# An attention block with adaptive layer norm on one core: the value products in blocks of four steps, the turned maxima behind a block, and low parts formed from PSUM

## The reference, cut to what matters

```python
sa, ca, ga, sb, cb, gb = silu(c) @ wmod           # six vectors of 256 per batch; ga, gb kept away from 0
h = layernorm(x) * (1 + ca) + sa
q, kv = h @ Wq.T, h @ Wkv_down.T                  # 8 heads of 64; keys and values come from a latent of 64
k, v = kv @ Wk_up.T, kv @ Wv_up.T
x = x + ga * (softmax(q k / 8) v) @ Wo.T          # per head, 1024 x 1024 scores
h2 = layernorm(x) * (1 + cb) + sb
x = x + gb * (h2 @ weight.T + pooled(h2) @ disha)
```

## Time and profile before, and how to read it

| | |
|---|---|
| median of 3 runs | 3259.14 us (3256.48 to 3263.53) |
| the profiled execution: its own time, its span | 3262.56 us, 3260.8 us |
| TensorE matmul, busy | 3175.0 us, 97% of the span |
| VectorE, ScalarE, GpSimd, busy | 67%, 52%, 79% |
| chain that ended last: TensorE's share | 92% |

### The profile page before, as it was taken

How to read it: one execution, slowest core, us unless ns; L and a number is a source line. 1 busy time by engine, 2 the same in 40 slices (tenths; PEclk the granted TensorE clock), 3 DMA queues, 4 the chain that set the end, 5 groups by cost and what they waited for, 6 DMA issues and landing times.

```text
span 3260.8 us, 44881 instructions
## 1 busy us (share of the span) xinstructions
PE 3175.0 (97%) x15398; PEld 1927.1 (59%) x15398; DVE 2200.4 (67%) x2542; ACT 1705.1 (52%) x3203; POOL 2584.8 (79%) x1513
## 2 busy tenths in 40 slices
PE   5999999999999999999999999999999999999995
PEld 3555656566566665665666565665656656666554
DVE  4657676776767767677776767767677776766652
ACT  1555555555555555555555555555555555555451
POOL 1778788887888878788887878878788887877882
PEclk7999999999999999999999999999999999999995
DMA  2111111111112011121111112111110111111111
GB/s 68 40 44 55 46 66 33 49 60 47 56 47 66 31 58 53 47 66 33 53 56 47 56 47 66 35 55 52 47 66 34 53 56 46 56 46 53 43 34 36
DMA packets 161746, 163.16 MB, mean 50 GB/s; under 512 B 58480, under 2 KB 109808, under 8 KB 161520
## 3 DMA queue, kind: packets, MB, share of 16 engines
q1 hardware_dynamic: 161520, 160.30, 15.0%
HBM read 74.66 MB, written 17.33 MB: 28 GB/s over the span
## 4 chain that ended last, share of the span: by engine, by line
PE 92%; DVE 5%; POOL 1%; issue 1%; ACT 1%; DMA 1%; SPq 0%; POOLq 0%; ACTq 0%; DVEq 0%
PE ps_mix L547 27%; PE ps_score L565 16%; PE ps_max L586 14%; PE ps_score L567 14%; PE ps_side L535 6%; PE ps_side L646 6%; PE ps_side L664 3%; PE ps_side L633 2%; DVE neg_max L984 1%; DVE w_out_lo L993 1%; POOL prob_sum L842 1%; PE ps_side L604 1%; DVE query L1027 1%; PE ps_side L653 1%; DVE h_lo L1017 1%
## 5 line engine op out<-in xcount | busy, mean ns | idle before, releaser
L842 POOL TENSOR_TENSOR prob_sum<-prob_sum,probs 128x1024 f32<-128x1024 f32 x768 | 1881.0, 2449 | 243.4 <-ACT probs L722 188.2
L984 DVE TENSOR_REDUCE neg_max<-ps_max 128x1 f32<-128x1024 f32 x1024 | 1247.9, 1220 | 755.3 <-PE ps_max L586 749.3
L722 ACT ACTIVATE probs<-ps_score 128x512 f32<-128x512 f32 x2048 | 1113.3, 598 | 969.0 <-PE ps_score L567 956.5
L547 PE MATMUL ps_mix<-probs,values 128*64 128x512 f32 x4096 | 991.6, 605 | 0.0
L565 PE MATMUL ps_score<-query,key_hi 128*128 128x512 f32 x2048 | 873.7, 427 | 1.1 <-ACT probs L722 1.1
L567 PE MATMUL ps_score<-query_m,key_lo 128*128 128x512 f32 x2048 | 805.0, 393 | 0.0
L586 PE MATMUL ps_max<-key_hi,query 128*128 128x512 f32 x2048 | 644.5, 396 | 8.3 <-DVE neg_max L984 5.4
L565 PEld LDWEIGHTS ps_score<-query,key_hi 128*128 128x128 f32 x2048 | 384.6, 188 | 326.7 <-issue 246.2
L547 PEld LDWEIGHTS ps_mix<-probs,values 128*64 128x64 f32 x4096 | 248.4, 136 | 477.8 <-issue 477.1
L842 POOL TENSOR_TENSOR prob_sum<-probs 128x1024 f32<-128x1024 f32 x128 | 328.9, 2570 | 228.6 <-ACT probs L722 228.3
L586 PEld LDWEIGHTS ps_max<-key_hi,query 128*128 128x128 f32 x2048 | 386.2, 189 | 102.3 <-DVE neg_max L984 10.9
(11 more groups left out here) (119 smaller groups left out, 2907.5 us busy)
## 6 DMA issues: line engine op xcount, KB each, us to landing
query_m<-query SPq DMA_DIRECT2D x128, 512.0 KB, 3.2
recip<-recip_scratch SPq DMA_DIRECT2D x256, 128.0 KB, 2.9
x_in<-in_L_attn_x_dram SPq DMA_DIRECT2D x32, 512.0 KB, 4.0
x_mid<-in_L_attn_x_dram SPq DMA_DIRECT2D x64, 256.0 KB, 4.5
out_dram<-x_mid SPq DMA_DIRECT2D x64, 256.0 KB, 2.2
denoms<-recip SPq DMA_DIRECT2D x512, 1.0 KB, 1.7
gates<-gates_scratch SPq DMA_DIRECT2D x16, 256.0 KB, 4.1
query_m<-max_row SPq DMA_DIRECT2D x128, 4.0 KB
```

The source lines that it names most:

```text
L547: last = nc.tensor.matmul(ps_mix[j * R:j * R + R, :], values[par][:, k, :], probs[:, s % RING, j * HALF:(j + 1) * HALF], start=(k == 0), s ...
L722: nc.scalar.activation(probs[:, s % RING, half * HALF:(half + 1) * HALF], ps_score[half], ACT.Exp, scale=SCALE).then_inc(exps_done, 1)
L842: nc.gpsimd.tensor_tensor(out=total[:, :], in0=before, in1=probs[:, s % RING, :], op=ALU.add).then_inc(adds_done, 1)
L984: nc.vector.tensor_reduce(neg_max[:, m:m + 1], ps_max[m % 2][:, :], AX_X, ALU.max, negate=True).then_inc(maxima_done, 1)
```

## The change

- `MIXED` goes from 2 to 4: the products of four steps run together, in the steps 1, 5, 9, ... of a slot, and there are 16 blocks in a slot instead of 32. `RING` goes from 4 to 6.
- `max_row` goes from the steps 1, 9, 17, ... to 5, 13, 21, ... (four steps later in a group), `denominator` from 3, 11, ... to 1, 9, ... (two steps earlier); `MIX_LAG` goes from 5 to 4. Both stand in a step with a block, as before.
- `norm_t`: ScalarE now writes `h_hi` and then, from SBUF, `h_rest` = shift - `h_hi`; VectorE forms `h_lo` = scale * PSUM + `h_rest` in the same step and frees `ps_side`. `norm2_t` likewise: two activations for `h2_hi`, two for `h2_rest`, then two operations of VectorE. The pieces `h2_split`, L1008, L1017 and `split_h2` are gone.
- Places in `PLAN` move: `norm_t` to (8, 12, 16, 20), `out_proj` to (10, 14, 18, 22, ...), `mixed_hi` to (6, 15, 24, 40), `norm2` to (18, 26, 38, 50), and the gating of the `ffn` weights to the steps 2, 3 and 5. `query`, `latent`, `values_t`, `norm2_t` and `ffn` keep their steps.
- The two `mixed` buffers become one of 11 rows, which the batches use in turn from either end; the weights staged at the start go to other tiles.

```diff
-RING = 4
+RING = 6
-SPREAD_LAG, RECIP_LAG, OUT_LAG, BACK_LAG, MIX_LAG = 1, 2, 2, 3, 5
-MIXED = 2
+SPREAD_LAG, RECIP_LAG, OUT_LAG, BACK_LAG, MIX_LAG = 1, 2, 2, 3, 4
+MIXED = 4
-OUT_GATES_LOAD, OUT_GATE, OUT_HI, OUT_LO = 44, 52, 54, (56, 59)
-FFN_GATE, FFN_HI, FFN_LO = (1, 8), (3, 9), (7, 11)
+OUT_GATES_LOAD, OUT_GATE, OUT_HI, OUT_LO = 44, 52, 54, (57, 61)
+FFN_GATE, FFN_HI, FFN_LO = (1, 2), (3, 3), (7, 5)
     "query": (40, 42, 50, 58, STEPS, STEPS + 2, STEPS + 4, STEPS + 6),
-    "norm_t": (8, 10, 16, 18),
+    "norm_t": (8, 12, 16, 20),
     "latent": (26, 32),
     "values_t": (54, 60),
-    "mixed_hi": (9, 16, 24, 40),
-    "mixed_lo": (10, 17, 25, 41),
-    "out_proj": (12, 14, 20, 22, 30, 36, 44, 46),
-    "norm2": (16, 25, 38, 49),
+    "mixed_hi": (6, 15, 24, 40),
+    "mixed_lo": (9, 17, 25, 41),
+    "out_proj": (10, 14, 18, 22, 30, 36, 44, 46),
+    "norm2": (18, 26, 38, 50),
     "norm2_t": (24, 34, 48, 56),
-    "h2_split": (25, 35, 49, 57),
     "ffn": (28, 38, 52, 62),
...
-        "max_row": STEPS - NT + 1 + NT * i,
-        "denominator": NT * (i + 1) + 3,
+        "max_row": STEPS - NT + 5 + NT * i,
+        "denominator": NT * (i + 1) + 1,
...
                         elif kind == "norm_t":
...
-                            for part, done in ((h_hi[:, f, cols], h_hi_done), (h_whole[:, i % 2, :], side_drained)):
-                                nc.scalar.activation(part, ps_side[:, :], ACT.Identity,
-                                                     scale=mod1[:, f:f + 1], bias=mod1[:, NF + f:NF + f + 1]).then_inc(done, 1)
+                            nc.scalar.activation(h_hi[:, f, cols], ps_side[:, :], ACT.Identity,
+                                                 scale=mod1[:, f:f + 1], bias=shift).then_inc(h_hi_done, 1)
+                            need_alone(act, h_hi_done, 2 * (2 * NF * b + i) + 1)
+                            nc.scalar.activation(h_rest[:, i % 2, :], h_hi[:, f, cols].bitcast(F32), ACT.Identity,
+                                                 scale=-1.0, bias=shift).then_inc(h_hi_done, 1)
...
                             for f in range(NF):
-                                last = nc.scalar.activation(h2_t[:, f, :], ps_side[:, f * CT * P:(f + 1) * CT * P], ACT.Identity,
-                                                            scale=mod2[:, f:f + 1], bias=mod2[:, NF + f:NF + f + 1])
-                            last.then_inc(side_drained, 1)
+                                nc.scalar.activation(h2_hi[:, f, :], ps_side[:, f * CT * P:(f + 1) * CT * P], ACT.Identity,
+                                                     scale=mod2[:, f:f + 1], bias=mod2[:, NF + f:NF + f + 1]).then_inc(h2_hi_done, 1)
+                            for f in range(NF):
+                                need_alone(act, h2_hi_done, 2 * NF * (CHUNKS * b + i) + NF + f)
+                                nc.scalar.activation(h2_rest[:, f, :], h2_hi[:, f, :].bitcast(F32), ACT.Identity,
+                                                     scale=-1.0, bias=mod2[:, NF + f:NF + f + 1]).then_inc(h2_hi_done, 1)
...
+                        elif kind == "norm2_t":
+                            need(dve, h2_hi_done, 2 * NF * (CHUNKS * b + i + 1))
+                            for f in range(NF):
+                                last = nc.vector.scalar_tensor_tensor(h2_lo[:, f, :], ps_side[:, f * CT * P:(f + 1) * CT * P],
+                                                                      mod2[:, f:f + 1], h2_rest[:, f, :], ALU.mult, ALU.add)
+                            last.then_inc(side_drained, 1)
```

More of the change, by code:

```diff
@@ L256, in adaln_block @@
         prob_total = recip
-        mixed = [sb(f"mixed{i}", [P, PAIRS, T]) for i in range(2)]
+        mixed = sb("mixed", [P, 2 * PAIRS + 3, HALF])
         mixed_hi = sb("mixed_hi", [P, PAIRS, CT * P], F32R)
@@ L606, in side_work @@
                     elif kind == "latent":
-                        need(pe, h_split, 2 * NF * b + NF * (i + 1))
+                        need(pe, side_drained, z.through("norm_t", NF * i + 1) + 1)
                         if first(z):
@@ L655, in side_work @@
                     elif kind == "ffn":
-                        need(pe, h2_split, CHUNKS * b + i + 1)
+                        need(pe, side_drained, z.through("norm2_t", i) + 1)
                         if i == 0:
@@ L700, in _ @@
             nc.scalar.activation(s_silu[:, 0, :, :], s_c, ACT.Exp, scale=-1.0).then_inc(exp_c_made, 1)
[L702 to L706, removed]
             act.wait_ge(fold_a_kept, 8)
@@ L728, in slot @@
                         need(act, group_done, GROUPS * zg.c + g + 1)
-                        nc.scalar.activation(mixed[zg.par][:, p, half * HALF:(half + 1) * HALF], ps_mix[:, :],
+                        if zg.has_o and p > half:
+                            need(act, mixed_split, CHUNKS * zg.o + 2 * (half + 1))
+                        nc.scalar.activation(mixed_block(zg.par, p, half), ps_mix[:, :],
                                              ACT.Copy).then_inc(group_evacuated, 1)
@@ L840, in add_probs @@
                     need(pool, adds_done, done)
-                before = probs[:, (s - 1) % RING, :] if k == 1 else total[:, :]
-                nc.gpsimd.tensor_tensor(out=total[:, :], in0=before, in1=probs[:, s % RING, :], op=ALU.add).then_inc(adds_done, 1)
+                now = STEPS * z.c + s
+                before = probs[:, (now - 1) % RING, :] if k == 1 else total[:, :]
+                nc.gpsimd.tensor_tensor(out=total[:, :], in0=before, in1=probs[:, now % RING, :], op=ALU.add).then_inc(adds_done, 1)
             def slot(z):
@@ L1013, in slot @@
                         statistics(z.n + 1, 0, AHEAD_STATS.index(s))
-                    for g in range(CHUNKS):
-                        if z.has_o and s == z.step("h2_split", g):
-                            need(dve, h2_hi_done, CHUNKS * z.o + g + 1)
-                            nc.vector.tensor_tensor(h2_lo[:, :, :], h2_t[:, :, :], h2_hi[:, :, :].bitcast(F32),
-                                                    ALU.subtract).then_inc(h2_split, 1)
                     for kind, i, b, w in z.at(s):
@@ L1034, in slot @@
                                                     key_hi[1 - z.par][:, cols].bitcast(F32), ALU.subtract).then_inc(side_drained, 1)
+                        elif kind == "norm_t":
+                            need(dve, h_hi_done, 2 * (2 * NF * b + i + 1))
+                            half, f = divmod(i, NF)
+                            cols = slice(half * HALF, (half + 1) * HALF)
+                            nc.vector.scalar_tensor_tensor(h_lo[:, f, cols], ps_side[:, :], mod1[:, f:f + 1], h_rest[:, i % 2, :],
+                                                           ALU.mult, ALU.add).then_inc(side_drained, 1)
+                        elif kind == "norm2_t":
[4 more added lines that the diff above has]
+                            last.then_inc(side_drained, 1)
                         elif kind == "out_proj":
```

46 lines of the change are left out of this document (20 added, 26 removed).

## The result

| | before | after |
|---|---|---|
| median (4 runs each, one chip) | 3261.34 us (3256.48 to 3263.89) | 3328.93 us (3322.27 to 3336.40) |
| ratio, 95% interval | | 1.021 [1.0183, 1.0237] |
| profiled execution: its own time, its span | 3262.56, 3260.8 us | 3336.40, 3334.6 us |

The change makes the kernel 68 us slower by the medians and 73.8 by the spans. The prediction had the sign, and its range (3224 to 3335) holds the time, but its size was +32 where +68 came.

The account below looks back on a forecast made before the run. TensorE, busy 97% of the span, bounds the kernel. Terms -88 -6 +62 +8 +8 +29 +3 +6 +10 sum to +32 us, 3291 us median; ends -5 to +70, own range 3255 to 3330, full range 3224 to 3335.

Parts of the forecast that it names:

- Part 1: TensorE's product blocks: two blocks in one save 0.35 us, over 252 blocks, -88 us.
- the hold-back of the first score matmul: After a wait, the first score matmul holds the second back by 0.34 us instead of 0.23: 0.11 per late drain.
- Part 2: Scores wait for ScalarE's exponentials where no block follows: query +62, latent +8, values +8, `norm2_t` +29, `mixed_hi` +3 us.
- `mixed_hi` at step 15 (+3): ScalarE's 1.06 us copy between exponentials, mostly covered by step 16's transposes: 0.2 us, 15 times, +3 us (0 to 9).
- The step that failed first: Steps with `out_proj` and `ffn`: VectorE drains them, they take 1.4 us of TensorE, nothing late; no cost.
- The step that failed second: Scaling at `MIX_LAG` 4 may hold VectorE, but the maxima queued behind have 3.6 us of cover; no cost.
- Part 3: Denominators two steps earlier use up group 6's 6.07 us margin: +6 us (0 to 15); an old query-drain wait goes: -6 us.
- Part 4: Low parts on VectorE: worth nothing in a slot; `ps_side` held longer at start and tail, +10 us (2 to 16).
- Rival B: GpSimd holds the steps; two groups a slot wait 2 us for additions, 60 us more: 3350; B and C together 0.12.
- A: Rival: late exponentials are absorbed, only saved blocks and small terms remain: -75 us, 3184 us; chance 0.12.
- A': Rival: late exponentials are partly absorbed, half the price: 3238 us; chance 0.12.
- C: Rival: blocks of four save only half and the waits stay: 44 us more, 3335; B and C together 0.12.

Follow-up runs that it names:

- Experiments 2 and 3: 2: changed kernel with five pairs of places exchanged, 3269.24 us; 3: changed kernel with an unused third copy of PSUM by ScalarE for five queries, 3368.82 us.
- experiment 6: Changed kernel with the low part of the ffn weights (`w_ffn_lo`) at step 13 instead of 5: 3325.72 us, ratio 1.02 to the kernel before.
- experiment 9: Changed kernel with blocks of two and the earlier kernel's places and lags, keeping low parts, ring of six, one `mixed` buffer: 3342.79 us, ratio 1.024.

## Why the prediction was right in sign and wrong in size

- **Part 1, blocks**: right where it was read. A block of four takes 3.65 us, and blocks with their ends save 60 us against 63.
- **Part 1 and 2, the hold-back of the first score matmul**: wrong by 9 us. I let each saved block save 0.1 and charged it back only behind late drains. It came back in the plain steps too: the second matmul starts over 0.29 us behind the first 43 times a slot, before and after alike.
- **Part 2, late exponentials**: right. Forecast and measured waits: query 0.69 and 0.70 to 0.72 (0.85 at step 8), latent 0.43 and 0.45, values 0.43 and 0.5, `norm2_t` 1.84 and 1.73. `mixed_hi` at step 15 (+3) shows nothing beyond the wait of a plain step. Experiments 2 and 3 confirm them from either side.
- **The step that failed first**: "`out_proj` and `ffn` are drained by VectorE ...: nothing late there". Nothing is late, but scores, exponential and scores again close in 1.38 us, and the step offers 1.39. The missing cover costs 0.08 of wait six times a slot, 7.8 us in the run, and most of the 9 us of hold-back above: some 17 us.
- **The step that failed second**: the scaling "may hold VectorE, but ... the maxima queued behind it have 3.6 us of cover". I did not add up what stands in that queue: two operations of 2.9 us. The transposes lose 7.6 us to it (experiment 6 takes them away), and the maxima of the steps 0, 8 and 48 about 8 more to VectorE (at the turn to slot 3 to the scaling's DMA and `w_out_lo`; the other slots' queues are not taken apart): 16 us. At a lag of four steps the scaling also waits 205.5 us for the reciprocals' DMA, 122 times, where it waited 12.9, four times.
- **Part 3, denominators**: the mechanism was right, the term mis-sized: 0.9 us a slot instead of 0.4. The new wait is 13.7 us where 6 were forecast, and the old one that goes is 7.8 where 6 were forecast: +6 instead of 0. Rival B was this wait at 2 us for two groups; it came at one group and under half the size.
- **Part 4**: nothing in a slot and 6.6 us at the start, as forecast (the tail gave nothing). But "worth nothing" holds behind the long blocks and in the new places; with blocks of two in the old places the same edit costs 78 us (experiment 9), which I had not seen.
- **The ends of the range**: the ends that stand with the terms add up to +1 and +62; the -5 and +70 of the sum have no working. That 3329 lies within the range owes to this width and to rival B's, not to the terms.
- **The rivals**: A and A' fell on the waits of step 4, 36 and the rest; C fell on the block's 3.65 us.

What stays open: why the wait of a plain step is there behind some pieces (the steps 16, 24, 32, 40, 48 and 0) and not behind others (12 and 20), and whether the additions of group 6 can be made earlier without the wait moving to VectorE. Blocks of four with the old low parts were not tried, so the saving of the blocks with nothing else changed stays open.

## What to carry to other kernels

A long instruction in the list of a packed engine is also a cover: before merging two of them, list every drain, subtraction and DMA that the vanishing one hid, in every queue, and give those places to work that no one waits for. Read the shortest loop between two engines, not only what is late: a step whose matmuls take just as long as the round trip of its one buffer has lost its cover already. And test the parts of such a change apart: here the new low parts cost nothing in a slot with the long blocks and new places and 78 us with the short blocks and old ones, and moving ten places in a table was worth 65 us.

## What the runs showed of the hardware that I had not expected

VectorE's subtraction and scaling of two SBUF operands take far longer beside a GpSimd addition: the scaling of 128x512 takes 748 ns on average before and 1526 after. In the kernel after, the 21 of its 128 that meet no addition take 693 ns on average, and the one at 699.78, which starts 0.01 us after a run of additions does, took 2.91 us. The new low parts, one operand of which lies in PSUM, do not slow down beside the same additions: those of 128x512 take 750 ns, the 37 that run mostly beside an addition as well as the 26 that meet none. Group rows of DVE in the kernel after:

```profile
L982 DVE TENSOR_TENSOR mixed<-mixed,recip 128x512 f32<-128x512 f32 x128 | 195.3, 1526 | 206.2 <-DMA recip<-recip_scratch 205.5
...
L1036 DVE SCALAR_TENSOR_TENSOR h_lo<-ps_side,mod,h_rest 128x512 fp32r<-128x512 f32 x64 | 48.0, 750 | 55.1 <-ACT h_rest L778 54.2
```

The old subtraction of the same size for `norm_t`, from two SBUF tiles, took 1678 ns on average. The Trainium skill ("SBUF — State Buffer", Who interferes with whom) states that a VectorE instruction with two SBUF inputs contends with a GpSimd instruction that reads SBUF, over a shared port pair that is locked exclusively, and that one with at most one SBUF input, outside the two-port modes, does not contend. Both rows agree.
